# Two graph layers on one core: the order of work in the passage from the first layer to the second

## The chip, the cores and the metric

The kernel runs on one NeuronCore of a Trainium2 chip. The metric is the device time of one execution in microseconds (us), as the median of several executions. "PE" is TensorE, "DVE" VectorE, "ACT" ScalarE, "POOL" GpSimd, "SP" the engine that here only issues transfers.

## What is computed

`x` is 4096 x 256, `adj` a symmetric 0/1 matrix of 4096 x 4096 (`deg` is its row sum, at least 1). Cut to what matters:

```python
x = layernorm(x + relu(((adj + I) @ x / deg + x) @ W + b))       # layer 0
type_sum = adj @ x                                                # layer 1, x is the new x
attn_a = sigmoid(concat(type_sum, x) @ Wa.T + ba)                 # attn_b: the same with Wb, bb
h = x @ W_sa
scores = (h @ a_left)[:, None] + (h @ a_right)[None, :]
e = where(adj != 0, exp(-leaky_relu(scores, 0.01)), 0)
x_a = (e / (e.sum(1) + 1e-5)) @ h
x_b = adj @ (x @ W_gcnb) + b_gcnb
x = layernorm(x + sigmoid(attn_a * x_a + attn_b * x_b))
```

## The kernel before, in words

Each engine runs a list of instructions that is written out by hand (`nc.Block`, one function for each engine). Semaphores `S[...]` order the engines among each other; each engine takes its own list in order, so an instruction that waits holds back all that stand behind it. There are T = 32 row tiles of 128 rows, and NP = 16 pairs of them.

**Layer 0** multiplies the adjacency with `y` (`sum_rows`, L1416) tile by tile. Behind each tile come, one to three tiles later, a transpose (`t_step`), the projection of the new tile with all weights of layer 1 (`p_step`, L1451), and on ACT `proj_copies`: `q` and `ex` (columns for the scores), `gb` (the part `g` of the projection that the adjacency multiplies), and the upper half of `h`. DVE makes the lower halves (`h_lo`, L958 and L960). Values that feed TensorE are kept as two float16 parts, high and low. `g_sums` and `forms_hi` and `forms_lo` (L948 to L953) make the sums of `g` for a pair of tiles.

**Layer 1** runs over 16 steps `s`, one for each 256 columns of the adjacency, in two slots that take turns. A step has two kinds of TensorE work:
- seven products M1 to M7 of a Strassen-like scheme (`product`, L1516), 16 matmuls each, whose adjacency operand is either the panel `pan` (M3, M4) or one of five byte-wise differences of it (`difference`, L967, written by DVE to `dd`). They are made one step ahead: `free_products` M3 and M4, `outer_products` M1 and M6, `onto_products` M2 and M5, `last_product` M7. ACT and DVE read them out: `low_m34`, `low_m1`, `low_m52`, `low_m67` on ACT, `middle`, `middle_m1`, `read_52`, `add_52`, `read_67`, `add_67` on DVE. PE may not overwrite a bank before it is read (`mid_read`, `m52_read`, `m67_read`).
- four chunks of `e @ h` (`e_chunk`, L1575), 48 matmuls each. A chunk passes through `exp_chunk` (ACT, 8 exponentials, L639), `mask_chunk` (DVE, L1141), `high_chunk` (ACT, L648) and `low_chunk` (DVE, L1148); the last one raises `elow_ready`, for which the `e_chunk` waits.

At a step's end DVE (`attend`, `statistics`), POOL (`pool_bias` L456, `pool_rstd` L462 and L466) and ACT (`gates`, `gated`, `sigmoid`, `norm`) finish the rows. `act_step`, `dve_step` and `pe_step` hold the order of a step; the steps 0, 1 and 2 are written out ahead of the loop, with `ramp` and `second` marking the first two calls.

**The passage.** Before the first exponential the kernel needs a bound on the scores over all rows: `nsr` and `NM` (L1070, L1072), a transpose on PE (L1547), the maximum `NMAX` (L1101), and `slb` (L1105). PE meanwhile works on the products of panel 0, whose last pair (NP - 1) needs the last tile's `g`:

```python
pe.wait_ge(S["forms_ready"], NP)
product(0, "M3", NP - 1, NP)
product(0, "M4", NP - 1, NP)
...
pe.wait_ge(S["hlo_ready"], T)
outer_products(0, 0)
```

## Time and profile before

| what | value |
|---|---|
| median of 3 executions | 867.2 us (866.87 to 869.27) |
| the profiled execution | 867.15 us |
| its span, first to last instruction | 865.0 us |
| PE busy | 851.7 us, 98% of the span |
| DVE busy | 668.3 us, 77% |
| ACT busy | 572.9 us, 66% |
| POOL busy | 181.2 us, 21% |
| mean granted TensorE clock | 0.999 |

The 2.15 us between the span and the time of that execution lie outside the instructions. Layer 0 ends and layer 1 begins at about 315 to 341 us. A time within a row is counted from the start of the span. In a timeline row the first number is the start, the second the time until the last of the merged instructions ends, and the bracket at the end the engine's idle time before it with what released it. Instructions of one engine overlap a little, so that from one start to the next it is slightly less than the duration.

### The profile page before, as it was taken

The numbers are of one execution on the slowest core, as the hardware profiler recorded it, in microseconds if no ns is written. First come the engines' busy times: TensorE is split into PE (matmuls) and PEld (weight loads), VectorE is DVE, ScalarE is ACT, GpSimd is POOL, SyncE is SP. The second block draws the span as 40 slices with busy tenths as digits, with TensorE's granted clock in tenths as the row PEclk, the third lists the DMA queues.
The fourth block names the chain that finished last, engine by engine and source line by source line (L and its number), as shares of the span: only waits on it lengthen the run. The fifth ranks groups of instructions, "written<-read, shape, count | busy, mean of one in ns | idle before, by whom it ended". The sixth has DMA issues, their size and how long they took to land.

```text
span 865.0 us, 20467 instructions
## 1 busy us (share of the span) xinstructions
PE 851.7 (98%) x7574; PEld 753.8 (87%) x7574; DVE 668.3 (77%) x1180; ACT 572.9 (66%) x1217; POOL 181.2 (21%) x181
## 2 busy tenths in 40 slices
PE   8999999999999998999999999999999999999997
PEld 7888888888888887888888888888888888888886
DVE  6697766656665558899988988987987978978963
ACT  5774645555554238989976886876876966967831
POOL 1003232223222311013122112212122032032031
PEclk9999999999999999999999999999999999999999
DMA  9989999989895642110221021021120120120001
GB/s 316 365 297 384 366 392 365 356 313 382 305 351 205 222 153 86 56 56 2 80 80 67 13 79 67 11 79 30 48 79 24 55 79 13 65 79 0 26 25 37
DMA packets 66649, 130.01 MB, mean 150 GB/s; under 512 B 5496, under 2 KB 29088, under 8 KB 62112
## 3 DMA queue, kind: packets, MB, share of 16 engines
q1 hardware_dynamic: 57392, 120.61, 39.0%
q10 hardware_dynamic: 9200, 8.64, 3.0%
q8 instruction: 36, 0.59, 0.3%
q14 instruction: 21, 0.17, 0.1%
HBM read 99.87 MB, written 29.36 MB: 149 GB/s over the span
## 4 chain that ended last, share of the span: by engine, by line
PE 80%; DVE 9%; issue 6%; ACT 4%; POOL 1%; DMA 0%; DVEq 0%; ACTq 0%; POOLq 0%; SPq 0%
PE ps L1575 27%; PE ps L1416 25%; PE ps L1516 18%; PE ps L1451 5%; PE ps L1398 3%; DVE ec L1141 2%; DVE em L1148 2%; ACT ec L639 2%; ACT em L648 1%; DVE dd L967 1%; PE ps L1383 1%; PE ps L1436 1%; PE ps L1374 0%; POOL sc L462 0%; DMA x1r<-x_scratch 0%
## 5 line engine op out<-in xcount | busy, mean ns | idle before, releaser
L1575 PE MATMUL ps<-fb,em 128*128 128x257 f16 x3072 | 347.5, 273 | 0.8 <-DVE em L1148 0.8
L1575 PEld LDWEIGHTS ps<-fb,em 128*128 128x128 f16 x3072 | 300.4, 98 | 38.8 <-issue 1.5
L1416 PE MATMUL ps<-y,codes 128*128 128x257 f16 (+1 forms) x2048 | 237.0, 273 | 0.0
L1416 PEld LDWEIGHTS ps<-y,codes 128*128 128x128 fp8e4 x2048 | 200.2, 98 | 25.9 <-DVE y L856 0.4
L639 ACT ACTIVATE ec<-slb,nsb 128x256 f32<-128x256 f32 x512 | 211.1, 497 | 0.0
L1148 DVE SCALAR_TENSOR_TENSOR em<-ec,em 128x2048 f16<-128x2048 f32 x64 | 147.3, 2302 | 20.9 <-ACT em L648 20.9
L648 ACT ACTIVATE em<-ec 128x2048 f16<-128x2048 f32 x64 | 122.0, 1908 | 60.4 <-PE ps L1575 51.3
L1141 DVE SCALAR_TENSOR_TENSOR ec<-ec,pan 128x2048 f32<-128x2048 f32 x64 | 147.2, 2300 | 3.2 <-issue 2.8
L1516 PE MATMUL ps<-zz,dd 128*128 128x256 f16 x768 | 89.4, 273 | 0.1
L462 POOL TENSOR_TENSOR sc<-sc,sc 128x2 f32<-128x2 f32 x15 | 36.6, 2438 | 244.6 <-DVE sc L1250 244.6
L1516 PEld LDWEIGHTS ps<-zz,dd 128*128 128x128 fp8e4 x768 | 75.1, 98 | 9.1 <-issue 0.4
L514 ACT ACTIVATE codes<-strip 128x1024 uint8<-128x1024 f32 x67 | 67.1, 1044 | 1.1
L456 POOL TENSOR_TENSOR w<-w,bgb 128x512 f32<-128x512 f32 x16 | 27.7, 1732 | 177.3 <-DVE w L1208 177.3
L967 DVE SCALAR_TENSOR_TENSOR dd<-pan 128x512 uint32<-128x512 uint32 (+2 forms) x85 | 64.2, 815 | 0.0
L1516 PE MATMUL ps<-fa,pan 128*128 128x260 f16 x512 | 60.0, 274 | 1.4 <-DVE zz L953 1.1
L1516 PE MATMUL ps<-fa,dd 128*128 128x260 f16 x512 | 59.6, 274 | 1.2 <-DVE m L1160 1.1
L569 ACT ACTIVATE q<-ps,sc 128x1 f32<-128x1 f32 x32 | 11.3, 352 | 72.8 <-PE ps L1451 72.8
L1516 PEld LDWEIGHTS ps<-fa,pan 128*128 128x128 fp8e4 x512 | 49.9, 98 | 8.5 <-DVE zz L953 1.4
L1516 PEld LDWEIGHTS ps<-fa,dd 128*128 128x128 fp8e4 x512 | 49.9, 98 | 8.3 <-issue 1.7
L983 DVE TENSOR_SCALAR lnst<-ps 128x1 f32<-128x1 f32 x32 | 5.0, 155 | 62.4 <-PE ps L1416 62.4
L554 ACT ACTIVATE x1t<-ps 128x256 f16<-128x256 f32 x32 | 12.2, 383 | 60.1 <-PE ps L1436 60.1
L684 ACT ACTIVATE ot<-sg,sc 128x256 f32<-128x256 f32 x30 | 16.4, 593 | 52.1 <-POOL sc L466 52.1
(153 smaller groups left out, 827.6 us busy)
## 6 DMA issues: line engine op xcount, KB each, us to landing
strip<-in_adj_dram SPq DMA_DIRECT2D x128, 512.0 KB, 7.7
a_scratch<-codes SPq DMA_DIRECT2D x16, 1024.0 KB, 9.6
pan<-a_scratch SPq DMA_DIRECT2D x16, 1024.0 KB, 4.9
x_scratch<-x ACTq DMA_DIRECT2D x32, 128.0 KB, 5.3
x1r<-x_scratch SPq DMA_DIRECT2D x16, 256.0 KB, 2.7
h_scratch<-hst ACTq DMA_DIRECT2D x30, 136.0 KB, 5.6
out_dram<-ot SPq DMA_DIRECT2D x15, 256.0 KB, 2.2
fb<-h_scratch SPq DMA_DIRECT2D x3, 1088.0 KB, 8.7
```

The costliest lines, as they stand in the source:

```text
L456: pool.tensor_tensor(w[:], w[:], bgb[:].unsqueeze(1).broadcast_to([P, 2, D]), ALU.add).then_inc(S["bias_ready"], 1)
L462: pool.tensor_tensor(sc1[:, RS2], sc1[:, VE2], sc[:, MH2], ALU.pow).then_inc(S["yrstd_ready"], 1)
L514: act.activation(codes_of(s), strip_of(s), ACT.Copy, scale=float(EDGE - NONE), bias=float(NONE)).then_inc(S["cast_act"], 1)
L639: e_ = act.activation(ec[:, c % ER, jj, :], slb[:, slot, :], ACT.Exp, scale=-(1 - SLOPE), bias=nsb[:, jb:jb + 1])
L648: act.activation(em[:, c, 0], ec[:, c % ER], ACT.Copy, scale=MU / EDGE_VAL).then_inc(S["ehigh_ready"], 1)
L967: return dve.scalar_tensor_tensor(out=o, in0=b, scalar=0x7f7f7f7f, in1=a, op0=ALU.bitwise_and, op1=ALU.bitwise_xor)
L1141: dve.scalar_tensor_tensor(out=ec[:, c % ER], in0=ec[:, c % ER], scalar=1.0, in1=pan[:, slot, c * CH:(c + 1) * CH, :].bitcast(F8), op0=ALU ...
L1148: dve.scalar_tensor_tensor(out=em[:, c, 1], in0=ec[:, c % ER], scalar=MU / EDGE_VAL, in1=em[:, c, 0], op0=ALU.mult, op1=ALU.subtract).then ...
L1416: mm = pe.matmul(ACC(n)[:, 0:cols], codes[:, qq % SLOTS, h, jb, e * P:(e + 1) * P].bitcast(F8), y[:, jb, part, 0:cols], start=(jb == 0 and ...
L1451: mm = pe.matmul(b, x1t[:, n % 2, x_part, k * P:(k + 1) * P], wps[:, k, w_part, c0:c1], start=(k == 0 and x_part + w_part == 0), stop=(k = ...
L1516: mm = pe.matmul(ps[:, bank, 0:2 * c], a.bitcast(F8), g, start=(p == 0), stop=(p == NP - 1))
L1575: mm = pe.matmul(PH(2 * m + e)[:, 0:HC], em[:, c, e_part, i, e * P:(e + 1) * P], fb[:, jb, h_part, 0:HC], start=(jb == 0 and e_part + h_pa ...
```

## The change

It touches only the passage and the steps 0 to 2; the loop over the other steps is as before.
- PE: the last pair's matmuls are split, so that what needs only the earlier pairs (or only `fa4`, with the new semaphore `fa_ready`) stands ahead; `onto_products` of step 0 waits for one difference less; the wait for the last tile's `h_lo` moves from ahead of `outer_products(0, 0)` to ahead of the fourth `e_chunk`.
- ACT: the last tile's `gb` is copied ahead of `q` and `ex`; `slc` and the last column of `nsb` move from DVE to ACT; the last `h` moves behind `low_m34(1)`; the first `high_chunk` becomes two halves behind the fourth and the fifth exponential of chunk 1; several `high_chunk`s move ahead of an `exp_chunk`, among them the one at the head of `act_step` with `ramp`.
- DVE: the differences of the last two pairs of panel 0 move ahead of the last `g_sums`; the first mask and the first low part become two halves each; `add_52` and `add_67` of step 0, the last `h_lo`, and some differences stand later; in step 1 `mask_chunk(1, 1, 2)` stands behind the five differences of panel 2.
- POOL: its first `pool_bias` is gone, and DVE does it (`first_bias`).

```diff
@@ -467,7 +467,6 @@
                                             two(MV2, 2)[:, e, 0:1], -1.0, ALU.mult, ALU.mult)
                 p_.then_inc(S["yshift_ready"], 1)
 
-            pool_bias(0)
             with pool.Fori(0, NPAN // 2 - 1) as k:
                 for i in range(2):
                     pool_bias(k * 2 + (i + 1))
...
@@ -625,6 +624,31 @@
                 if more:
                     cast(2)
             assert next(todo, None) is None
+
+            def last_projection():
+
+                n = T - 1
+                act.wait_ge(S["proj_done"], T)
+                act.activation(gb[:, n % 2, :], BG(n)[:, 0:GC], ACT.Copy, scale=GSC).then_inc(S["g_ready"], 1)
+                act.activation(q[:, n:T], BG(n)[:, GC + 3:WG], ACT.Exp, scale=sc[:, QSC], bias=sc[:, QB]
+                               ).then_inc(S["q_ready"], 1)
+                act.activation(ex[:, n, :], BG(n)[:, GC:WG], ACT.Copy, scale=sc[:, EXS]).then_inc(S["ex_ready"], 1)
+                act.wait_ge(S["ex_ready"], T)
+                act.copy(slc[:], ex[:, :, 2]).then_inc(S["sl_ready"], 1)
+                act.activation(nsb[:, n:T], ex[:, n, 3:4], ACT.Copy, scale=-(1 - SLOPE)).then_inc(S["slb_ready"], 1)
+                forms_hi(NP - 1)
+
+            def last_h():
+
+                n = T - 1
+                act.wait_ge(S["q_ready"], T)
+                act.activation(qa[:, n:T], q[:, n:T], ACT.Copy, scale=1.0 / PROJ).then_inc(S["qa_ready"], 1)
+                act.wait_ge(S["qa_ready"], T)
+                h = h_place(n)
+                act.activation(h[:, 0, D:HC], q[:, n:T], ACT.Copy, scale=KAPPA)
+                act.activation(h[:, 0, 0:D], BH, ACT.Copy, scale=qa[:, n:T]).then_inc(S["hhi_ready"], 1)
+
+            last_projection()
 
             def exp_chunk(s, slot, c, nth=0, first=False, behind={}):
...
 
+            def first_half_high(i):
+
+                half = slice(i * CH // 2, (i + 1) * CH // 2)
+                act.wait_ge(*((S["masked"], 1) if i else (S["half_masked"], 1)))
+                h_ = act.activation(em[:, 0, 0, half], ec[:, 0, half], ACT.Copy, scale=MU / EDGE_VAL)
+                h_.then_inc(S["ehigh_ready" if i else "half_high"], 1)
+
+            def first_half_highs(u):
+
+                low_m67(u, first=True)
+                act.wait_ge(S["acc_done"], T)
+                for j in range(SLOTS):
+                    act.wait_ge(codes_out[j], 32 * len(range(j, NQ, SLOTS)))
+                first_half_high(0)
...
@@ -715,8 +754,11 @@
             def act_step(s, m, nth, ramp=False, second=False):
 
                 n = 1 - m
+                if ramp:
+                    high_chunk(s, 2)
                 exp_chunk(s + 1, n, 0, nth)
-                high_chunk(s, 2)
+                if not ramp:
+                    high_chunk(s, 2)
                 if ramp:
                     low_m34(s + 1)
                 elif second:
@@ -752,34 +794,28 @@
                 act.wait_ge(S[sem], n)
             act.wait_ge(S["slb_ready"], 2)
             exp_chunk(0, 0, 0, first=True, behind={4: low_m34, 5: low_m1, 7: lambda u: low_m52(u, first=True)})
-            exp_chunk(0, 0, 1, first=True, behind={6: lambda u: low_m67(u, first=True)})
-            act.wait_ge(S["acc_done"], T)
-            for j in range(SLOTS):
-                act.wait_ge(codes_out[j], 32 * len(range(j, NQ, SLOTS)))
-            high_chunk(0, 0, True)
+            exp_chunk(0, 0, 1, first=True, behind={4: first_half_highs, 5: lambda u: first_half_high(1)})
             act.wait_ge(S["m52_read"], 1)
             low_m34(1)
-
-            exp_chunk(0, 0, 2, first=True)
-            high_chunk(0, 1, True)
+            last_h()
+            exp_chunk(0, 0, 2, first=True, behind={5: lambda u: high_chunk(u, 1, True)})
             low_m1(1)
             for j in range(X1RING):
                 act.wait_ge(x1_out[j], 16 * T // X1RING)
-            act.wait_ge(S["proj_done"], T)
             exp_chunk(0, 0, 3, first=True)
+            high_chunk(0, 2, True)
             exp_chunk(1, 1, 0, 1)
             low_m52(1)
-            high_chunk(0, 2, True)
             high_chunk(0, 3, True)
+            high_chunk(1, 0)
             exp_chunk(1, 1, 1)
             act.wait_ge(S["arg_ready"], 1)
             act.activation(rr[:], tb[:], ACT.Exp).then_inc(S["rr_ready"], 1)
             gates(0, 0)
             gated(0, 0, first=True)
-            high_chunk(1, 0)
             low_m67(1)
+            high_chunk(1, 1)
             exp_chunk(1, 1, 2)
-            high_chunk(1, 1)
             exp_chunk(1, 1, 3)
             act_step(1, 1, 2, ramp=True)
...
 
-            def forms_lo(p):
+            def forms_lo(p, last=False):
 
                 dve.wait_ge(S["ghi_ready"], p + 1)
                 dve.tensor_tensor(fa4[:, p, 0:2, P + 2:2 * P + 4], gb[:, 0:3:2, 0:P + 2], fa4[:, p, 0:2, 0:P + 2],
                                   ALU.subtract)
-                dve.tensor_tensor(fa4[:, p, 2:4, P + 2:2 * P + 4], gb[:, 1:3, P:GC], fa4[:, p, 2:4, 0:P + 2],
-                                  ALU.subtract)
+                f_ = dve.tensor_tensor(fa4[:, p, 2:4, P + 2:2 * P + 4], gb[:, 1:3, P:GC], fa4[:, p, 2:4, 0:P + 2],
+                                       ALU.subtract)
+                if last:
+                    f_.then_inc(S["fa_ready"], 1)
...
@@ -1061,25 +1099,18 @@
             x1t_lo(6)
             forms_lo(2)
             cast(2)
-            for n in range(SPREAD + 1, T + 3):
+            for n in range(SPREAD + 1, T + 2):
                 more = n // PT + 1 < NQ and n < T
                 if n - 1 < T:
                     degree(n - 1)
-                if n == T + 2:
-                    dve.wait_ge(S["ex_ready"], T)
-                    dve.tensor_scalar(nsr[:], ex[:, :, 3], -1.0, None, ALU.mult).then_inc(S["nsr_ready"], 1)
-                    dve.wait_ge(S["nsr_ready"], 1)
-                    dve.tensor_reduce(sc[:, NM], nsr[:], AX, ALU.max).then_inc(S["nsr_max"], 1)
-                    dve.tensor_copy(slc[:], ex[:, :, 2]).then_inc(S["sl_ready"], 1)
...
                 if n - 1 < T:
                     stats(n - 1)
-                if n % 2 == 0 and n < T + 2:
+                if n % 2 == 0:
                     forms_lo((n - 3) // 2)
                 if more:
...
             assert next(todo, None) is None
+            for op in DIFF_ORDER:
+                difference(0, op, NP - 2, NP).then_inc(S["diff_ready"], 1)
+            dve.wait_ge(S["ex_ready"], T - 1)
+            dve.tensor_scalar(nsr[:, 0:T - 1], ex[:, 0:T - 1, 3], -1.0, None, ALU.mult).then_inc(S["nsr_ready"], 1)
+            dve.tensor_scalar(nsb[:, 0:T - 1], ex[:, 0:T - 1, 3], -(1 - SLOPE), None, ALU.mult)
+            dve.wait_ge(S["nsr_ready"], 1)
+            dve.tensor_reduce(nsr[:, T - 1:T], nsr[:, 0:T - 1], AX, ALU.max).then_inc(S["nsr_ready"], 1)
             g_sums(dve, NP - 1)
-            dve.tensor_scalar(nsb[:], ex[:, :, 3], -(1 - SLOPE), None, ALU.mult).then_inc(S["slb_ready"], 1)
-
+            dve.wait_ge(S["ex_ready"], T)
+            dve.wait_ge(S["nsr_ready"], 2)
+            dve.scalar_tensor_tensor(out=sc[:, NM], in0=ex[:, T - 1, 3:4], scalar=-1.0, in1=nsr[:, T - 1:T],
+                                     op0=ALU.mult, op1=ALU.max).then_inc(S["nsr_max"], 1)
             dve.wait_ge(S["nmt_done"], 1)
             dve.tensor_reduce(sc[:, NMAX], ps[:, 5, P:2 * P], AX, ALU.max).then_inc(S["nmax_ready"], 1)
             for m in range(2):
...
-            for op in DIFF_ORDER:
-                difference(0, op, NP - 2, NP).then_inc(S["diff_ready"], 1)
+            forms_lo(NP - 1, last=True)
 
             def row_ends():
 
-                h_lo(T - 1)
                 dve.wait_ge(S["slt_done"], 1)
                 dve.tensor_scalar(slrow[:], ps[0:T, 5, 0:P], sc[0:T, NMAX], None, ALU.min
@@ -1147,6 +1184,29 @@
                 gate(dve, S["ehigh_ready"], s * NCH + c + 1, "passed_dve")
                 dve.scalar_tensor_tensor(out=em[:, c, 1], in0=ec[:, c % ER], scalar=MU / EDGE_VAL, in1=em[:, c, 0],
                                          op0=ALU.mult, op1=ALU.subtract).then_inc(S["elow_ready"], 1)
+
+            def first_half_mask(i):
+
+                half = slice(i * CH // 2, (i + 1) * CH // 2)
+                dve.wait_ge(S["exp_done"], 1)
+                dve.scalar_tensor_tensor(out=ec[:, 0, half], in0=ec[:, 0, half], scalar=1.0,
+                                         in1=pan[:, 0, half, :].bitcast(F8), op0=ALU.min, op1=ALU.mult
+                                         ).then_inc(S["masked" if i else "half_masked"], 1)
+
+            def first_half_low(i):
+
+                half = slice(i * CH // 2, (i + 1) * CH // 2)
+                dve.wait_ge(*((S["ehigh_ready"], 1) if i else (S["half_high"], 1)))
+                l_ = dve.scalar_tensor_tensor(out=em[:, 0, 1, half], in0=ec[:, 0, half], scalar=MU / EDGE_VAL,
+                                              in1=em[:, 0, 0, half], op0=ALU.mult, op1=ALU.subtract)
+                if i:
+                    l_.then_inc(S["elow_ready"], 1)
+
+            def first_bias():
+
+                dve.wait_ge(S["comb_ready"], 1)
+                dve.tensor_tensor(w[:], w[:], bgb[:].unsqueeze(1).broadcast_to([P, 2, D]), ALU.add
+                                  ).then_inc(S["bias_ready"], 1)
 
             def some_differences(u, slot, ops, done=NPROD):
...
@@ -1318,35 +1378,41 @@
             middle(0)
             middle_m1(0)
             some_differences(1, 1, DIFF_ORDER[0:2], done=4)
-            mask_chunk(0, 0, 0)
+            first_half_mask(0)
             read_67(0)
+            first_half_mask(1)
             row_ends()
             read_52(0, first=True)
+            for i in range(2):
+                first_half_low(i)
+            mask_chunk(0, 0, 1)
+            some_differences(1, 1, DIFF_ORDER[2:4], done=6)
             for i in range(HRING):
                 dve.wait_ge(h_out[i], 16 * len(range(i, T - 2, HRING)))
             add_52(0, first=True)
             add_67(0)
-            low_chunk(0, 0)
-            mask_chunk(0, 0, 1)
-            some_differences(1, 1, DIFF_ORDER[2:], done=NPROD + 1)
             middle(1)
             low_chunk(0, 1)
             mask_chunk(0, 0, 2)
+            some_differences(1, 1, DIFF_ORDER[4:], done=NPROD + 1)
             middle_m1(1)
+            h_lo(T - 1)
+            low_chunk(0, 2)
             mask_chunk(0, 0, 3)
-            low_chunk(0, 2)
+            mask_chunk(1, 1, 0)
+            low_chunk(0, 3)
+            low_chunk(1, 0)
             row_factors()
-            low_chunk(0, 3)
-            mask_chunk(1, 1, 0)
-            sums_52(1)
-            low_chunk(1, 0)
+            first_bias()
+            read_52(1)
+            mask_chunk(1, 1, 1)
+            add_52(1)
             denominators()
-            mask_chunk(1, 1, 1)
             sums_67(1)
-            mask_chunk(1, 1, 2)
             low_chunk(1, 1)
             dve.wait_ge(panel_in[0], 32)
             some_differences(2, 0, DIFF_ORDER)
+            mask_chunk(1, 1, 2)
             mask_chunk(1, 1, 3)
             low_chunk(1, 2)
...
@@ -1542,23 +1608,26 @@
             pe.wait_ge(S["g_ready"], T - 1)
             pe.wait_ge(S["diff_ready"], NDIFF)
             product(0, "M2", 0, early, bank=FIRST_52[1])
-            pe.wait_ge(S["g_ready"], T)
+            pe.wait_ge(S["diff_ready"], 2 * NDIFF)
+            product(0, "M1", early, NP - 1)
+            product(0, "M6", early, NP - 1)
+            pe.wait_ge(S["ex_ready"], T)
             pe.wait_ge(S["nsr_max"], 1)
             pe.transpose(ps[:, 5, P:2 * P], sc[:, NM].broadcast_to([P, P]), ident[:]).then_inc(S["nmt_done"], 1)
             product(0, "M5", 0, early, bank=FIRST_52[0])
             pe.wait_ge(S["sl_ready"], 1)
             pe.wait_ge(S["nmax_ready"], 1)
             pe.transpose(ps[0:T, 5, 0:P], slc[:], ident[:]).then_inc(S["slt_done"], 1)
-            pe.wait_ge(S["forms_ready"], NP)
+            pe.wait_ge(S["fa_ready"], 1)
             product(0, "M3", NP - 1, NP)
             product(0, "M4", NP - 1, NP)
-            pe.wait_ge(S["diff_ready"], NDIFF + 1)
-            product(0, "M1", early, NP)
-            pe.wait_ge(S["diff_ready"], NDIFF + 2)
-            product(0, "M6", early, NP)
-            pe.wait_ge(S["diff_ready"], 2 * NDIFF)
-            product(0, "M2", early, NP, bank=FIRST_52[1])
-            product(0, "M5", early, NP, bank=FIRST_52[0])
+            product(0, "M2", early, NP - 1, bank=FIRST_52[1])
+            product(0, "M5", early, NP - 1, bank=FIRST_52[0])
+            pe.wait_ge(S["forms_ready"], NP)
+            product(0, "M1", NP - 1, NP)
+            product(0, "M6", NP - 1, NP)
+            product(0, "M2", NP - 1, NP, bank=FIRST_52[1])
+            product(0, "M5", NP - 1, NP, bank=FIRST_52[0])
...
@@ -1622,15 +1691,22 @@
                 e_chunk(s, m, 3)
                 last_product(s, m)
 
-            pe.wait_ge(S["hlo_ready"], T)
             outer_products(0, 0)
             pe.wait_ge(S["m52_read"], 1)
             pe.wait_ge(S["slrow_ready"], 1)
             for c in range(NCH):
                 pe.wait_ge(fb_in[c], 16)
+                if c == NCH - 1:
+                    pe.wait_ge(S["hlo_ready"], T)
                 e_chunk(0, 0, c)
-                if c < 2:
-                    (onto_products, last_product)[c](0, 0)
+                if c == 0:
+                    pe.wait_ge(S["mid_read"], 3)
+                    pe.wait_ge(S["diff_ready"], 3 * NDIFF - 1)
+                    product(1, "M2")
+                    product(1, "M5")
+                if c == 1:
+                    pe.wait_ge(S["diff_ready"], 3 * NDIFF)
+                    last_product(0, 0)
             e_chunk(1, 1, 0)
             free_products(1, 1, 2)
             e_chunk(1, 1, 1)
```

## Rows read from the trace of the kernel before

**Rows 1.** The page: the span and PE's total (us, share, instructions).
```profile
span 865.0 us, 20467 instructions
PE 851.7 (98%) x7574; PEld 753.8 (87%) x7574; DVE 668.3 (77%) x1180; ACT 572.9 (66%) x1217; POOL 181.2 (21%) x181
```

**Rows 2.** Busy time by stretch: length, PE, PEld, DVE, ACT, POOL, clock, DMA.
```profile
458.88:859.00 400.12, 399.84 (x3632) 355.29 (x3632) 332.97 (x427) 286.51 (x565) 81.64 (x52) 1.00 0.14 47
```

**Rows 3.** Timeline of PE, from the last projection to step 3.
```profile
323.39 1.49 PE L1451 MATMUL ps<-wps,x1t 128*128 128x262 f16 x12
...
329.33 0.40 PE L1516 MATMUL ps<-fa,pan 128*128 128x260 f16 x2 [1.14 <-DVE zz L953]
...
330.86 1.95 PE L1516 MATMUL ps<-fa,pan 128*128 128x260 f16 x16 [0.24 <-DVE m L1160]
...
340.93 5.44 PE L1575 MATMUL ps<-fb,em 128*128 128x257 f16 x48 [0.80 <-DVE em L1148]
...
415.35 3.66 PE L1516 MATMUL ps<-zz,dd 128*128 128x256 f16 x32
...
458.88 3.71 PE L1516 MATMUL ps<-fa,dd 128*128 128x260 f16 x32 [1.15 <-DVE m L1160]
```

**Rows 4.** The chain that ended last, 377 to 459 us: start, us, what.
```profile
398.68 0.79 DVE em L1148
...
432.22 2.64 POOL sc L462
...
458.15 0.35 DVE m L1160
```

**Rows 5.** Timeline of ACT, 324 to 382 us.
```profile
324.92 0.35 ACT L569 ACTIVATE q<-ps,sc 128x1 f32<-128x1 f32 x1 [2.47 <-PE ps L1451]
...
327.91 1.69 ACT L639 ACTIVATE ec<-slb,nsb 128x256 f32<-128x256 f32 x4
...
371.22 6.48 ACT L639 ACTIVATE ec<-slb,nsb 128x256 f32<-128x256 f32 x16
377.61 1.90 ACT L648 ACTIVATE em<-ec 128x2048 f16<-128x2048 f32 x1
...
381.81 1.91 ACT L648 ACTIVATE em<-ec 128x2048 f16<-128x2048 f32 x1 [2.05 <-DVE ec L1141]
```

**Rows 6.** Timeline of DVE, 330 to 415 us.
```profile
330.38 0.43 DVE L1160 TENSOR_TENSOR m<-ps,lc 128x260 f32<-128x260 f32 x1 [0.42 <-ACT lc L691]
...
335.29 0.42 DVE L1200 TENSOR_TENSOR s<-ps,lc 128x256 f32<-128x256 f32 x1
335.63 0.15 DVE L958 SCALAR_TENSOR_TENSOR fb<-q,fb 128x1 f16<-128x1 f32 x1
...
336.10 0.33 DVE L1115 TENSOR_SCALAR slrow<-ps,sc 32x128 f32<-32x128 f32 x1
...
337.10 0.23 DVE L1189 TENSOR_TENSOR sc<-s,m 128x2 f32<-128x2 f32 x2 [0.28 <-DVE s L1177]
...
338.38 2.28 DVE L1148 SCALAR_TENSOR_TENSOR em<-ec,em 128x2048 f16<-128x2048 f32 x1
340.59 3.36 DVE L1141 SCALAR_TENSOR_TENSOR ec<-ec,pan 128x2048 f32<-128x2048 f32 x1
...
354.74 2.29 DVE L1148 SCALAR_TENSOR_TENSOR em<-ec,em 128x2048 f16<-128x2048 f32 x1 [1.09 <-ACT em L648]
...
364.69 2.29 DVE L1148 SCALAR_TENSOR_TENSOR em<-ec,em 128x2048 f16<-128x2048 f32 x1 [1.13 <-ACT em L648]
...
379.40 2.28 DVE L1141 SCALAR_TENSOR_TENSOR ec<-ec,pan 128x2048 f32<-128x2048 f32 x1
...
400.89 0.68 DVE L1241 SCALAR_TENSOR_TENSOR sg<-sg,x1r 128x512 f32<-128x512 f32 x1
...
414.26 4.17 DVE L967 SCALAR_TENSOR_TENSOR dd<-pan 128x512 uint32<-128x512 uint32 x5
```

**Rows 7.** Timeline of POOL, 319 to 342 us.
```profile
338.65 3.14 POOL L456 TENSOR_TENSOR w<-w,bgb 128x512 f32<-128x512 f32 x1 [19.04 <-DVE w L1208]
```

More of the change, by code:

```diff
@@ L232, in build @@
             "sl0_out", "ex_ready", "alpha_ready", "slb_ready", "masked", "exp_done", "ehigh_ready", "elow_ready",
-            "diff_ready", "prod_done", "low_m34", "low_m1", "low_m52", "low_m67", "mid_read", "m52_read", "m67_read",
+            "fa_ready", "half_masked", "half_high", "diff_ready", "prod_done", "low_m34", "low_m1", "low_m52", "low_m67", "mid_read", "m52_read", "m67_read",
             "comb_ready", "ext_ready", "bias_ready", "echunk_done", "tile_done", "epsr_ready",
@@ L1063, in _ @@
             cast(2)
-            for n in range(SPREAD + 1, T + 3):
+            for n in range(SPREAD + 1, T + 2):
                 more = n // PT + 1 < NQ and n < T
@@ L1067, in _ @@
                     degree(n - 1)
-                if n == T + 2:
-                    dve.wait_ge(S["ex_ready"], T)
-                    dve.tensor_scalar(nsr[:], ex[:, :, 3], -1.0, None, ALU.mult).then_inc(S["nsr_ready"], 1)
-                    dve.wait_ge(S["nsr_ready"], 1)
-                    dve.tensor_reduce(sc[:, NM], nsr[:], AX, ALU.max).then_inc(S["nsr_max"], 1)
-                    dve.tensor_copy(slc[:], ex[:, :, 2]).then_inc(S["sl_ready"], 1)
-                if n < T + 2:
-                    h_lo(n - 3)
+                h_lo(n - 3)
                 if n - 1 < T:
@@ L1105, in _ @@
             dve.tensor_scalar(slb[:], slb[:], sc[:, NMAX], None, ALU.min).then_inc(S["slb_ready"], 1)
-            forms_lo(NP - 1)
-            for op in DIFF_ORDER:
-                difference(0, op, NP - 2, NP).then_inc(S["diff_ready"], 1)
+            forms_lo(NP - 1, last=True)
             def row_ends():
-                h_lo(T - 1)
                 dve.wait_ge(S["slt_done"], 1)
```

## The prediction

> **What bounds the kernel now.** I read the page first. PE is busy for 851.7 of 865.0 us [rows 1], so no order of work can win more than about 13 us. PE's work itself is the same before and after, matmul for matmul. So I looked for PE's idle time from the passage on, in its timeline [rows 3]: 1.14 us ahead of the last pair (for `zz`), 0.24 (for `middle`), 0.80 ahead of the first `e_chunk` (for the first low part), and then 1.15 at 458.88, far behind the passage, again for a `middle`. From there to 859 us PE is busy for 399.84 of 400.12 us [rows 2]. So the end of the kernel is the start at 458.88 plus a constant, and the change is worth what it moves that start.
>
> Then I asked the chain of waits what holds 458.88, and this decides my forecast [rows 4]. Between 381.81 and 458.88 the chain does not touch PE. It runs through ACT (from the `high_chunk` at 381.81 on [rows 5], ACT without a pause of note to the `high_chunk` that releases DVE's low part at 398.68), then DVE to 432 us, then POOL's `pool_rstd` (432.22, 2.64 us), ACT, and DVE to `middle` at 458.15. PE has only 1.15 us to spare against that chain. Two clocks run side by side: PE's, and the ACT and DVE chain's. A gain counts only if both move; if only PE's moves, PE waits later.
>
> **PE's clock.** The first copy of ACT behind the last projection stays at 324.92 [rows 5]. With `gb` ahead of `q` (0.35) and `ex`, the `g_sums` and the forms come about 0.5 us earlier. `slb` does not: it needs `ex`, now behind `gb`, then NM, transpose and maximum. The shorter last reduction and the moved `slc` pay that back, so the first exponential starts at about 327.75 instead of 327.91 (before, the end of `forms_hi` held it). Four exponentials at 0.40 each (sixteen took 6.48 [rows 5]) bring ACT to `low_m34` at 329.35. PE, which before started the last pair at 329.33, is now through with it by then and no longer late. So `middle(0)` starts about 0.5 us earlier than its 330.38 [rows 6], at 329.87, and PE goes on at 330.3 instead of 330.86 [rows 3]: of PE's 1.4 us of idle time, 1.0 stays, now in one piece ahead of `product(1, "M3")`.
>
> PE's next 80 matmuls, less the wait for `h_lo` that stood among them (some 0.3 us), bring it to the first `e_chunk` at 339.1. The first low part decides next. DVE does two differences and the first half mask by 333.6 and then waits in `read_67`, because `low_m67` needs M7 finished: 330.3 + 32 matmuls at 0.11 = 333.8, 334.0 with the last one's tail; copy and hand-over 0.5: 334.55, against 335.29 before [rows 6]. From there: `read_67` 0.34, a half mask 1.13 (half of the 2.21 from 338.38 to 340.59 and a small fixed part; bounds 1.1 and 1.3), `slrow` 0.25, `read_52` 0.33, two half lows 2.26: DVE is free at 338.85, its data ready at 338.95. Before, with the `h_lo` (0.47 from 335.63 to 336.10) and the additions (1.28 from 337.10 to 338.38) ahead, that was 338.38 + 2.28 = 340.66 [rows 6]. PE starts its `e_chunk` at 339.25 instead of 340.93 [rows 3], 1.7 us earlier. Up to the end of step 1 each chunk's low part is ready ahead of PE by this sum (the closest is chunk 3 of step 0, 359.8 for 360.8), so PE's clock stands at -1.65 us.
>
> **The clock of ACT and DVE.** DVE did in 41.1 us, from 340.59 until `mask_chunk(1, 1, 3)` ended at 381.7 [rows 6], what it now starts at 338.85. The differences: the mask at 340.59 took 3.36 where others take 2.28, while POOL's `pool_bias` ran (338.65, 3.14 us [rows 7]); without POOL that is -1.08. In sentences that the sum can do without: the Trainium skill (SBUF — State Buffer, "Who interferes with whom") says that a DVE instruction with two SBUF inputs and a POOL instruction that reads SBUF lock each other out, and the trace agrees with 1.08 us. The moved bias costs DVE 0.55 (512 elements; the nearest row is `statistics`' 0.68, 400.89 [rows 6]; bounds 0.45 and 0.7). The two waits for ACT at 354.74 and 364.69 (1.09 and 1.13 [rows 6]) go: by my count the new order leaves 0.4 of them, ahead of `low_chunk(0, 2)`. The additions and the last `h_lo` move in: +1.28 and +0.47. In all 41.1 - 1.08 + 0.55 - 2.22 + 0.4 + 1.28 + 0.47 = 40.5: `mask_chunk(1, 1, 3)` ends at 379.35, 2.3 us earlier than before. So far the change does well.
>
> But the change swaps two things that meet here. `mask_chunk(1, 1, 2)` now stands behind the five differences, directly ahead of `mask_chunk(1, 1, 3)`, so it ends at 379.35 - 2.2 = 377.15; before it stood ahead of `low_chunk(1, 1)`. And ACT now puts `high_chunk(1, 2)`, which needs that mask, ahead of `exp_chunk(2, 0, 0)`. Before, ACT ran the two exponential chunks from 371.22 to 377.6 without a pause and took the `high_chunk` at 377.61 [rows 5] with its mask done. Now ACT has its last exponential done at 374.5 (by a count of its own list: the `high_chunk` ahead of `exp_chunk(1, 1, 2)` is released by a mask that ends at 366.3, 1.8 for it, 6.4 for two exponential chunks) and stands idle for 2.6 us until 377.2. Then, with nothing left to overlap: `high_chunk` 1.8, `exp_chunk` 3.2, `low_m34` 0.25, and it is at the `high_chunk(1, 3)` at 382.45, which before started at 381.81 [rows 5]. From there to `low_chunk(2, 1)` of DVE at 398.68 [rows 4] nothing changes (16.87 us, ACT's own work). So this clock comes out at 399.3, **+0.65 us**, although DVE was 2.3 us ahead.
>
> **What is late next.** Behind `low_chunk(2, 1)` DVE worked without a pause of note; its differences for step 3 began at 414.26 [rows 6], now 414.9. PE wants the first of them for `outer_products` at 415.35 - 1.65 = 413.7 [rows 3] and gets it at 415.6: a new idle time of some 2 us, at L1516, that eats PE's gain. From there PE has its old place plus 0.3. POOL and ACT follow DVE's +0.65, and `middle` starts at about 458.7, so PE goes on at 459.5. The sum against the profiled execution is 867.15 + 0.65 = 867.8; the median shown lies 0.05 above that execution: **867.9 us**. This is inside 0.3% (2.6 us), about what a measurement of this kernel can tell from no change.
>
> The other edits cost nothing that lasts: the last `h` is ready near 351 and wanted at 360.8; the panel's transfer is issued with the mask of chunk 3, about 1.7 us later than before, and lands about 10 us before its use; `pool_bias(1)` still takes its 1.08 from DVE, in the same stretch as before, and is in the sum.
>
> **The rivals.**
> - *DVE's lead survives.* If mask 2 is ready in time for ACT, or my sum for DVE is 3 us too long, the later chain moves with PE's clock: -1.65, and the 1.15 at 458.88 shrinks too, at most -2.8: 864.4 to 865.6. For it: DVE is 2.3 us ahead at 379 by my own sum, and the half instructions and the bias could be shorter. Against it: the 22.1 us of ACT work in a row from `high_chunk(1, 2)` on are rows, not guesses.
> - *Slower by a clock drop.* PE would stand idle for 1.0 us at 329.3 and 2 us at 413.7, longer than any gap in this stretch before. If the granted clock fell to 1.2 GHz behind one, an `e_chunk` of 5.28 us would take 10.5, and the end would be 5 us later beyond DVE's cover: 872. Against it: gaps of 1.14 and 1.15 us left the clock at 1.00 [rows 2, 3]. It decides only if the gap is long enough. The Trainium skill (TensorE: Matmul & The Clock Gate, "HAM oscillation — how this bites in real kernels") warns of idle gaps in which the clock drops to half; no row here shows one.
> - *The chain gets later than I count.* A further wait of ACT on DVE ahead of 377.2 (halves at 1.3, bias at 0.7) adds up to 1 us: 869.0. It is the upper end of my own case.
> - *Nothing moves.* The two clocks cancel exactly: 867.2, inside my own case.
>
> **How the numbers follow.** My case (ACT idle ahead of `high_chunk(1, 2)`, end between -0.8 and +1.9 us): 0.74, own range 866.4 to 869.1. DVE's lead survives: 0.19, of which 0.07 reach beyond 2.6 us. Clock drop: 0.03; a longer delay of the chain that I don't see: 0.04. So faster by over 0.3% 0.07, within 0.86, slower 0.07. The range takes my case and the upper half of the first rival: 865.2 to 869.6.
>
> **What would show it.** Right: PE's first `e_chunk` at 339.3 and its idle time ahead of it gone; DVE's first mask of chunk 1 at 2.28 us; ACT idle for 2 to 3 us, released by a mask (L1141's successor), ahead of a `high_chunk` near 377; low part (2, 1) at 399.3; a new gap of PE of about 2 us near 414, released by a difference. Wrong: no such gap near 414, or the gap at 458 gone; then the first rival holds. A granted clock under 1.00 near 330 or 415 would be the second.

## The result and the profile after

The changed kernel takes 868.6 us in the median of 22 executions, the kernel before 867.5 beside it: ratio 1.0013, 95% interval 1.0007 to 1.0019. That is 1.1 us more, clear of noise, and under the 0.3% of the forecast's middle class. I had forecast +0.65 us. The trace after is that of one execution of 868.78 us; where I give a number of a trace below, it comes from one execution of each kernel.

The page of the kernel after, span and totals:

```profile
span 866.7 us, 20471 instructions
PE 851.2 (98%) x7574; PEld 753.7 (87%) x7574; DVE 668.2 (77%) x1183; ACT 573.9 (66%) x1220; POOL 178.5 (21%) x180
```

The timeline of PE after (start, length, instruction, idle time before it and its releaser), in the lines that answer to [rows 3]:

```profile
323.92 1.49 PE L1517 MATMUL ps<-wps,x1t 128*128 128x262 f16 x12
...
331.00 1.95 PE L1582 MATMUL ps<-fa,pan 128*128 128x260 f16 x16 [0.89 <-DVE m L1220]
...
340.17 5.44 PE L1644 MATMUL ps<-fb,em 128*128 128x257 f16 x48 [0.21 <-DVE em L1200]
...
416.76 3.65 PE L1582 MATMUL ps<-zz,dd 128*128 128x256 f16 x32 [2.26 <-DVE dd L1005]
...
460.54 3.71 PE L1582 MATMUL ps<-fa,dd 128*128 128x260 f16 x32 [1.39 <-DVE m L1220]
```

One thing first: the last projection starts at 323.92 here and at 323.39 before. The code up to there is the same, and in the traces of this study that start lies between 322.9 and 324.6 whatever the kernel. So 0.53 of the 1.7 us between the two spans has nothing to do with the change, and I count every time from now on from the start of the last projection.

Counted so, the first `e_chunk` came 1.29 us earlier (16.25 for 17.54), and then PE lost it all: 2.26 us at 416.76, waiting for a difference (L1005), where before it waited for nothing, and again 1.39 at 460.54 for `middle` (1.15 before). That last start, the one that sets the end, comes at 136.62 for 135.49: **+1.13 us**, which is the measured 1.1. Why DVE was late is in ACT's timeline after, for [rows 5]:

```profile
369.26 6.48 ACT L663 ACTIVATE ec<-slb,nsb 128x256 f32<-128x256 f32 x16
378.21 1.91 ACT L672 ACTIVATE em<-ec 128x2048 f16<-128x2048 f32 x1 [2.47 <-DVE ec L1178]
380.03 3.29 ACT L663 ACTIVATE ec<-slb,nsb 128x256 f32<-128x256 f32 x8
383.22 0.35 ACT L730 COPY lc<-ps 128x260 f32<-128x260 f32 x1
383.48 1.91 ACT L672 ACTIVATE em<-ec 128x2048 f16<-128x2048 f32 x1
```

After two exponential chunks ACT stands still for 2.47 us until the mask of chunk 2 is done, and only then come the `high_chunk`, the third exponential chunk and `high_chunk(1, 3)`. Before, ACT ran from 371.22 to 379.5 without that pause [rows 5]. DVE's timeline after shows both sides of it, in the lines for [rows 6]:

```profile
335.43 0.42 DVE L1260 TENSOR_TENSOR s<-ps,lc 128x256 f32<-128x256 f32 x1 [1.06 <-ACT lc L752]
...
339.83 2.27 DVE L1178 SCALAR_TENSOR_TENSOR ec<-ec,pan 128x2048 f32<-128x2048 f32 x1
...
364.09 0.69 DVE L1208 TENSOR_TENSOR w<-w,bgb 128x512 f32<-128x512 f32 x1
...
371.71 4.17 DVE L1005 SCALAR_TENSOR_TENSOR dd<-pan 128x512 uint32<-128x512 uint32 x5
375.80 4.48 DVE L1178 SCALAR_TENSOR_TENSOR ec<-ec,pan 128x2048 f32<-128x2048 f32 x2
...
383.46 2.29 DVE L1178 SCALAR_TENSOR_TENSOR ec<-ec,pan 128x2048 f32<-128x2048 f32 x1 [0.90 <-ACT ec L663]
...
400.35 2.29 DVE L1185 SCALAR_TENSOR_TENSOR em<-ec,em 128x2048 f16<-128x2048 f32 x1 [1.42 <-ACT em L672]
```

The mask at 339.83 takes 2.27 us, not 3.36. The five differences (371.71) stand ahead of the two masks (375.80). The masks end at 380.28, which is 1.9 us earlier than before counted from the projection; but DVE then waits for ACT, and at 400.35 it is 1.14 us later.

### The profile page after: what moved, and what is told of

Read it like the earlier page. It is cut to its first block, busy times and chain, and to the rows that moved or that the text cites. A ratio compares the mean times of both kernels' runs of the same rounds, so it can differ in the third digit from the quotient of the medians.

```text
span 866.7 us, 20471 instructions
## 1 busy us (share of the span) xinstructions
PE 851.2 (98%) x7574; PEld 753.7 (87%) x7574; DVE 668.2 (77%) x1183; ACT 573.9 (66%) x1220; POOL 178.5 (21%) x180
## 4 chain that ended last, share of the span: by engine, by line
PE 78%; DVE 10%; issue 5%; ACT 4%; DMA 2%; POOL 1%; SPq 0%; DVEq 0%; ACTq 0%; POOLq 0%
PE ps L1644 27%; PE ps L1482 25%; PE ps L1582 18%; PE ps L1517 5%; DVE em L1185 2%; DVE ec L1178 2%; PE ps L1464 2%; ACT em L672 1%; DMA xs<-in_x_dram 1%; ACT ec L663 1%; DVE dd L1005 1%; PE ps L1502 1%; DVE sc L859 1%; PE ps L1449 0%; POOL sc L462 0%
## 5 line engine op out<-in xcount | busy, mean ns | idle before, releaser
L672 ACT ACTIVATE em<-ec 128x2048 f16<-128x2048 f32 x63 | 120.2, 1908 | 59.4 <-PE ps L1644 50.2
L1185 DVE SCALAR_TENSOR_TENSOR em<-ec,em 128x2048 f16<-128x2048 f32 x63 | 143.9, 2286 | 20.2 <-ACT em L672 20.2
L1178 DVE SCALAR_TENSOR_TENSOR ec<-ec,pan 128x2048 f32<-128x2048 f32 x63 | 143.8, 2285 | 5.1 <-ACT ec L663 2.5
L1005 DVE SCALAR_TENSOR_TENSOR dd<-pan 128x512 uint32<-128x512 uint32 (+2 forms) x85 | 65.3, 827 | 0.0
L456 POOL TENSOR_TENSOR w<-w,bgb 128x512 f32<-128x512 f32 x15 | 24.8, 1653 | 178.1 <-DVE w L1268 178.1
```

Source lines behind the costliest of these rows:

```text
L456: pool.tensor_tensor(w[:], w[:], bgb[:].unsqueeze(1).broadcast_to([P, 2, D]), ALU.add).then_inc(S["bias_ready"], 1)
L672: act.activation(em[:, c, 0], ec[:, c % ER], ACT.Copy, scale=MU / EDGE_VAL).then_inc(S["ehigh_ready"], 1)
L1005: return dve.scalar_tensor_tensor(out=o, in0=b, scalar=0x7f7f7f7f, in1=a, op0=ALU.bitwise_and, op1=ALU.bitwise_xor)
L1178: dve.scalar_tensor_tensor(out=ec[:, c % ER], in0=ec[:, c % ER], scalar=1.0, in1=pan[:, slot, c * CH:(c + 1) * CH, :].bitcast(F8), op0=ALU ...
L1185: dve.scalar_tensor_tensor(out=em[:, c, 1], in0=ec[:, c % ER], scalar=MU / EDGE_VAL, in1=em[:, c, 0], op0=ALU.mult, op1=ALU.subtract).then ...
```

## The experiments

My theory: two clocks, PE's own and that of ACT and DVE; the second sets the end, and one meeting in it (late mask, early `high_chunk`) throws the gain away. Rivals: the loss lies elsewhere in DVE's work; or PE's total work sets the end. "M2 of step 4" is the start of PE's `onto_products` near 458, the one that sets the end; both columns of times count from the last projection.

| kernel | ratio, 95% interval | first `e_chunk` | M2 of step 4 |
|---|---|---|---|
| before | 1 | 17.54 | 135.49 |
| after | 1.0013 (1.0007 to 1.0019) | 16.25 | 136.62 |
| e1_exp_first | 0.9984 (0.9975 to 0.9993) | 16.29 | 134.02 |
| e2_mask_first | 0.9985 (0.9976 to 0.9994) | 16.24 | 134.01 |
| e11_both_undone | 0.9980 (0.9971 to 0.9989) | 16.28 | 134.05 |
| e9_before_high_first | 1.0001 (0.9992 to 1.0010) | 17.54 | 135.54 |
| e10_before_both | 1.0038 (1.0024 to 1.0051) | 17.55 | 138.92 |
| e3_before_bias | 0.9989 (0.9980 to 0.9998) | 17.54 | 134.65 |
| e4_before_m52 | 0.9983 (0.9974 to 0.9992) | 17.53 | 134.18 |
| e5_pe_8 | 1.0002 (0.9993 to 1.0011) | 17.54 | 135.49 |
| e6_pe_24 | 1.0016 (1.0006 to 1.0025) | 17.53 | 136.69 |
| e7_whole_chunk | 1.0034 (1.0023 to 1.0046) | 17.46 | 137.78 |
| e8_exp_m52 | 0.9965 (0.9952 to 0.9977) | 16.25 | 132.47 |
| e12_early_reads | 0.9956 (0.9943 to 0.9970) | 15.86 | 132.09 |

### The meeting, undone in the changed kernel

e1, in `act_step`:

```diff
-                if ramp:
-                    high_chunk(s, 2)
                 exp_chunk(s + 1, n, 0, nth)
-                if not ramp:
-                    high_chunk(s, 2)
+                high_chunk(s, 2)
```

> The changed kernel with one edit undone: at the head of the ramp step ACT takes exp_chunk(2, 0, 0) again ahead of high_chunk(1, 2). My theory (ACT's 2.5 us of idle time ahead of that high_chunk makes the whole later chain late): the idle time is filled by the exponentials, high_chunk(1, 3) starts about 2.4 us earlier (near 381 instead of 383.5), low_chunk(2, 1) too, PE's 2.3 us gap near 414 ahead of outer_products goes, and the end comes 2.4 us earlier than in the changed kernel: 1.3 us under the kernel before (0.9985), with a gap of PE of about 1.1 us left near 458. Rival (the loss lies in the front of the passage, in DVE's own later work, and this order only moves the idle time about): the time stays 1.1 us above the kernel before.

e2, in DVE's list:

```diff
+            mask_chunk(1, 1, 2)
             dve.wait_ge(panel_in[0], 32)
             some_differences(2, 0, DIFF_ORDER)
-            mask_chunk(1, 1, 2)
             mask_chunk(1, 1, 3)
```

> The changed kernel with the other half of the same meeting undone: DVE takes mask_chunk(1, 1, 2) again ahead of the five differences of panel 2; ACT's order stays as changed. My theory: the mask is then ready when ACT has done exp_chunk(1, 1, 3) (near 375.8), ACT's idle time falls from 2.5 to about 0.2 us, and the end comes about 2.2 us earlier than in the changed kernel, 1.1 us under the kernel before (0.9987). DVE may wait up to 0.8 us for the exponentials of that mask, which costs the end nothing. Rival (DVE is the one that is late, so its order doesn't matter for the sum): 1.1 us above the kernel before, as the changed kernel.

e11 has both edits.

> The changed kernel with both parts of the meeting undone. My theory: either one alone cures the wait (each measured 1.3 to 1.5 us under the kernel before), so both together give the same, 0.9983 to 0.9985. Rival (two separate losses): the gains add, 4 us under the kernel before (0.9955).

Each alone takes 2.6 us off the changed kernel (136.62 to 134.0; I expected 2.4 and 2.2), and both together no more. So it is one loss, and it needs both sides. ACT's timeline of e1 shows the pause filled:

```profile
369.64 9.68 ACT L663 ACTIVATE ec<-slb,nsb 128x256 f32<-128x256 f32 x24
379.23 1.90 ACT L672 ACTIVATE em<-ec 128x2048 f16<-128x2048 f32 x1
```

and that of e2 the mask in time:

```profile
368.89 6.48 ACT L663 ACTIVATE ec<-slb,nsb 128x256 f32<-128x256 f32 x16
375.27 1.90 ACT L672 ACTIVATE em<-ec 128x2048 f16<-128x2048 f32 x1
```

### The meeting, put into the kernel before

e9 moves only ACT's `high_chunk(1, 2)` ahead of `exp_chunk(2, 0, 0)`; e10 also puts `mask_chunk(1, 1, 2)` behind the five differences.

> The kernel before with ACT's part of the meeting alone: high_chunk(1, 2) ahead of exp_chunk(2, 0, 0); DVE's order as before, with mask_chunk(1, 1, 2) ahead of the differences. My theory (the order costs only together with the late mask): the mask is done near 373.2 and ACT gets there at 374.4, so it does not wait, and the high part of chunk 3 stays at 381.8 behind its own mask: no change (1.0000, 0.2 us either way). Rival (ACT's order is bad by itself): 1 us or more longer.

> The kernel before with both parts of the meeting: mask_chunk(1, 1, 2) behind the five differences on DVE, and high_chunk(1, 2) ahead of exp_chunk(2, 0, 0) on ACT; nothing else of the change. My theory: the mask ends near 379.9, ACT stands idle from 374.4 to 380, and with 22.1 us of ACT's work from there low_chunk(2, 1) starts near 402.1 instead of 398.7: the end comes 3.4 us later (1.0039), with a gap of PE of 1 to 2 us near 416. Rival (PE or another wait behind absorbs part of it): 1 us or less.

e9: no change. e10: +3.43 us at M2 of step 4, for 3.4 expected (its median is 2.9 us over that of the kernel before), with a long pause of ACT:

```profile
379.69 1.91 ACT L648 ACTIVATE em<-ec 128x2048 f16<-128x2048 f32 x1 [5.42 <-DVE ec L1144]
```

The pause of 5.42 us stands in place of the one of 2.05 us that ACT had at 381.81 [rows 5]; the difference is the 3.4 us. So these two moves of the change cost 3.4 us by themselves. In the changed kernel they cost 2.6 (136.62 less 134.02): DVE comes to the mask earlier there, and the pause of 2.47 us stands in place of none in e1. The rest of the change wins 1.4 (e11), and the sum is the loss of 1.1. The mask's move alone was not put into the kernel before; in the changed kernel e1 is that case, and it costs nothing there. PE's timeline of e10 holds something I come back to:

```profile
407.08 3.71 PE L1519 MATMUL ps<-fa,pan 128*128 128x260 f16 x32 [0.74 <-DVE s L1182]
...
418.23 5.24 PE L1519 MATMUL ps<-zz,dd 128*128 128x256 f16 x32 [2.16 <-DVE dd L970]
423.31 5.44 PE L1578 MATMUL ps<-fb,em 128*128 128x257 f16 x48
```

### Which clock sets the end

e5 and e6 put more work on PE in the kernel before (8 and 24 small transposes of 0.11 us), and e4 takes DVE's late wait away. The edit of e5 and e6, shown with e5's number, and behind it that of e4:

```diff
                 if c < 2:
                     (onto_products, last_product)[c](0, 0)
+                if c == 1:
+                    for _ in range(8):
+                        pe.transpose(ps[:, 7, 384:512], ident[:], ident[:])
```

> The kernel before with 8 transposes more on PE (of the unit matrix into an unused part of a bank, 0.11 us each, 0.9 us in all) ahead of the third e_chunk of step 0. It measures PE's slack against the chain of ACT and DVE. My theory (1.15 us of slack at 458): the time stays, the gap at 458 shrinks to about 0.3 us. Rival (every microsecond of PE counts): 0.9 us longer (1.0010).

> As the run with 8, with 24 transposes more on PE (2.6 us). My theory: the first 1.15 us are free, the gap at 458 is gone, and 1.5 us remain (1.0017). Rival (every microsecond of PE counts): 2.6 us longer (1.0030).

```diff
-                    norm(s - 2)
                     low_m52(s)
+                    norm(s - 2)
```

> The kernel before with an edit of the loop: ACT takes low_m52(s) ahead of norm(s - 2). It is there to test the chain behind the passage: at 437 us ACT waits 5.4 us for POOL in norm, and DVE waits 2.15 us for the low_m52 behind it. My theory (that chain sets PE's start at 458.88): DVE comes 2.2 us earlier, PE's gap of 1.15 us goes, and the end comes 1.1 us earlier (0.9987), no more, as PE has no other gap. Rival (the end is set by something else, as PE's total work from the passage on): no change.

PE in e5, at the start that sets the end, with a gap still there though PE worked 0.9 us more:

```profile
458.89 3.71 PE L1516 MATMUL ps<-fa,dd 128*128 128x260 f16 x32 [0.54 <-DVE m L1160]
```

The gap fell by 0.61 us and not by 0.9. The other 0.28 went into two small waits of PE further ahead (0.18 us before the third `e_chunk` of step 0, 0.10 before the second of step 1), which are gone in e5.

In e6 the end moved by 1.2 us of the 2.6 (1.4 by the medians), near the 1.5 expected, but partly by another way than I wrote. PE's delay reached ACT through the product that `low_m1` reads, so the chain itself became later, as ACT's timeline of e6 shows:

```profile
387.20 0.27 ACT L696 COPY lc<-ps 128x128 f32<-128x128 f32 x1 [1.10 <-PE ps L1516]
```

Before, ACT waited for POOL in `norm`, and DVE for the `low_m52` behind it (ACT's timeline, then DVE's):

```profile
437.15 1.09 ACT L684 ACTIVATE ot<-sg,sc 128x256 f32<-128x256 f32 x2 [5.36 <-POOL sc L466]
438.15 0.35 ACT L706 COPY lc<-ps 128x260 f32<-128x260 f32 x1
...
438.65 0.43 DVE L1179 TENSOR_TENSOR s<-ps,lc 128x260 f32<-128x260 f32 x1 [2.15 <-ACT lc L706]
```

In e4 ACT does `low_m52` and then waits for POOL:

```profile
431.91 0.35 ACT L706 COPY lc<-ps 128x260 f32<-128x260 f32 x1
437.36 1.09 ACT L684 ACTIVATE ot<-sg,sc 128x256 f32<-128x256 f32 x2 [5.10 <-POOL sc L466]
```

DVE's `read_52` follows its low part without the 2.15 us pause, PE's gap at M2 of step 4 is gone, and the end comes 1.3 us earlier in the trace and 1.5 by the medians (1.1 expected). The bracket of 1.15 us understates that gap: from one start to the next PE lost 1.31 us there (457.57, which is 5.28 behind the `e_chunk` at 452.29, to 458.88). The passage is untouched in e4. PE had slack and the chain had none.

### Parts of the change

e3 is the kernel before with `pool_bias(0)` taken out and `first_bias()` behind `row_factors()` on DVE.

> The kernel before with one part of the change alone: the first bias on DVE (behind row_factors) instead of POOL. My theory: the mask of chunk 1 takes 2.28 us instead of 3.36, the bias costs DVE 0.6 later, DVE and ACT come 0.45 us earlier from there on, and as their chain sets the end, the end comes 0.4 to 0.5 us earlier (0.9995). Rival (PE's clock sets the end): no change, PE's gap at 458 stays 1.15 us or shrinks without gain. Second rival (the stretched mask has another cause than POOL): it stays at 3.36 us, and the kernel loses 0.6 us.

DVE's timeline of e3, beside 3.36 in [rows 6]:

```profile
340.75 2.28 DVE L1140 SCALAR_TENSOR_TENSOR ec<-ec,pan 128x2048 f32<-128x2048 f32 x1
...
357.10 0.68 DVE L1153 TENSOR_TENSOR w<-w,bgb 128x512 f32<-128x512 f32 x1
```

The stretched mask was POOL's doing: 1.08 us back for 0.6. The gain was 0.84 us in the trace, 0.4 more than the sum. Those 0.4 appear in step 1 between `read_67` and `add_67`, where DVE now goes on 0.56 us after the start of `read_67` instead of 0.92. That is so in every kernel here without POOL's first bias, the changed one too, and its cause stays open.

e7 is the changed kernel with the first chunk whole again.

> The changed kernel with the first chunk whole again (one mask, one high part behind chunk 1's exponentials, one low part), all else as changed. My theory: the halves serve PE's first e_chunk only. Without them the first low part waits for one whole mask and one whole high part in a row: the first e_chunk starts 1 to 2 us later than in the changed kernel (near 341.5), a gap of 1 to 2 us of PE opens ahead of it, DVE and ACT come about 1 us later as well, since DVE's next mask stands behind that low part, and the end is 0.5 to 1.5 us above the changed kernel. Rival (DVE and ACT make up for it in the waits that they have until 377): the end stays that of the changed kernel, because only the late chain counts.

```profile
337.84 2.29 DVE L1185 SCALAR_TENSOR_TENSOR em<-ec,em 128x2048 f16<-128x2048 f32 x1 [2.33 <-ACT em L672]
```

Without halves DVE stands still for 2.33 us, and PE's first `e_chunk` comes 1.21 us later than in the changed kernel. M2 of step 4 comes 1.16 us later too: DVE did not catch up behind it. By the medians e7 is 1.7 us slower than the changed kernel, a little over the 1.5 that I expected at most, and the traced execution is the fastest of its seven; the trace can't show where the others lost more. The halves serve both clocks, not PE's alone.

### The version that beats both

e8 joins e1's edit and e4's to the changed kernel; e12 also moves the first reads of the product banks:

```diff
-            exp_chunk(0, 0, 0, first=True, behind={4: low_m34, 5: low_m1, 7: lambda u: low_m52(u, first=True)})
+            exp_chunk(0, 0, 0, first=True, behind={3: low_m34, 4: low_m1, 6: lambda u: low_m52(u, first=True)})
```

> The changed kernel with exp_chunk(2, 0, 0) ahead of high_chunk(1, 2) again and with low_m52(s) ahead of norm(s - 2) in the loop. My theory (two clocks: the late chain of ACT and DVE, and PE's own, which the passage moved 1.2 us earlier): with both late waits gone the end is set by PE alone, 2.4 us under the kernel before (0.9973), no gap near 414 nor near 458. Rival (the two edits cure the same wait): 1.2 to 1.3 us under the kernel before.

> The version with exp_chunk(2, 0, 0) first and low_m52 ahead of norm, with one more edit: low_m34, low_m1 and low_m52 of the first product set stand one exponential earlier on ACT. It is aimed at PE's last gap in the passage (0.90 us, for middle). My theory (PE alone sets the end of that version, so what its gap loses counts in full): middle starts 0.4 us earlier, PE's gap falls from 0.9 to 0.5 us, the end comes 0.4 us earlier, 3.3 us under the kernel before (0.9961). Rival (the first e_chunk waits for the first low part, which is not earlier): the gap moves to the first e_chunk, no change against 0.9965.

In e8 PE has no gap from the first `e_chunk` to step 4, and in e12 the gap for `middle` fell from 0.90 to 0.49. PE's timeline of e12:

```profile
330.50 1.95 PE L1579 MATMUL ps<-fa,pan 128*128 128x260 f16 x16 [0.49 <-DVE m L1217]
...
339.67 5.44 PE L1641 MATMUL ps<-fb,em 128*128 128x257 f16 x48 [0.21 <-DVE em L1197]
...
455.90 3.71 PE L1579 MATMUL ps<-fa,dd 128*128 128x260 f16 x32
```

e12 takes 863.8 us beside 867.3 of the kernel before: 0.9956 (0.9943 to 0.9970), the fastest here. Against e8 it is 0.38 us ahead in the trace, as expected; the two intervals overlap, so that step is seen in the trace only. e8 gained 3.0 us where I expected 2.4. The first `e_chunk` gives 1.29 of it, the gap near 458 gives 1.31 counted from start to start, and the rest are three small waits of the kernel before in steps 0 and 1 (0.18, 0.18 and 0.10 us), which went as well.

## Why the prediction was right, point by point

- **The end is the start of M2 near 458 plus a constant.** Right. It is 1.13 us later in the trace, the time 1.1.
- **PE's clock.** The first `e_chunk` was to come 1.7 us earlier and came 1.29 earlier. The mis-sized term is the hand-over at `low_m67`: `read_67` started at 334.90 (335.43 less 0.53) for 334.55. PE's run with M7 in it started 0.17 later than in my sum (330.47 for 330.3), and `read_67` came 0.2 later after it than I allowed.
- **The clock of ACT and DVE.** The stretched mask, gone: right. The bias takes 0.69, or 0.60 from its start to the next, for 0.55. `mask_chunk(1, 1, 3)` ended at 379.75 for 379.35, the same 0.35 to 0.4 carried on. That the stretch between came out at 40.45 for 40.5 is partly luck: DVE waited 0.75 us for ACT in it (0.58 and 0.17) where I had left 0.4, and the 0.36 between `read_67` and `add_67`, which I did not foresee, paid that back.
- **The meeting.** Right in place and size: ACT idle for 2.47 us (2.6 forecast), 22.14 us from that `high_chunk` to DVE's low part at 400.35 (22.1 forecast). My count of ACT's own list was 0.7 us short (its exponentials ended at 375.21 for 374.5), which cost nothing, as the mask ended later still. e1, e2, e10 and e11 show that this meeting is the cause, and e9 that ACT's half of it is harmless alone.
- **PE's new gap near 414.** Right: 2.26 us, released by a difference.
- **The sum.** +0.65 forecast, +1.13 in the trace. Of the missing 0.48, 0.35 arose by `read_67`; the rest is in small terms behind it, as `read_52` (0.40 for 0.33) and the hand-over from the mask to ACT (0.13 for 0.05).
- **Rival, DVE's lead survives.** Not in this kernel, but it is what e1 and e2 are: 1.4 us under the kernel before.
- **Rival, clock drop.** Not in the profiled execution: the granted clock was 1.00 on both sides of the 2.26 us gap. In e10 it happened (below), and the mean clocks below suggest that it happened in other executions of the changed kernel. I gave it 0.03, too little for a drop, and I was wrong about its price too: in e10 ACT's and DVE's chain covered it.

## What to carry to other kernels

Follow the chain of waits back from the last gap of the engine that seems to bound the kernel. If the chain does not touch that engine for a long stretch (here 77 us), a gap of that engine closed ahead of the stretch is worth nothing unless the chain comes earlier too. Two harmless reorderings on two engines can be harmful together: check each moved consumer against the place of its producer in the other engine's new list. And measure slack by adding work: 8 small transposes told that PE had a microsecond to spare (ratio 1.0002, 0.9993 to 1.0011).

## What the runs showed of the hardware

In e10 PE waited 0.74 us at 407 and 2.16 us at 416, and the 32 matmuls behind took 5.24 us where the same 32 take 3.65. The rows by stretch of e10 (length, PE, PEld, DVE, ACT, POOL, granted clock, DMA) show why:

```profile
410.00:416.00 6.00, 6.00 (x56) 5.15 (x53) 6.00 (x3) 5.87 (x15) 6.00 (x2) 1.00 0.00 0
416.00:418.00 2.00, 0.07 (x1) 0.00 (x0) 1.82 (x5) 2.00 (x3) 0.50 (x2) 1.00 0.00 0
418.00:420.00 2.00, 1.77 (x9) 1.27 (x10) 2.00 (x3) 2.00 (x6) 1.21 (x1) 0.53 0.00 0
420.00:422.00 2.00, 2.00 (x13) 1.46 (x12) 2.00 (x4) 2.00 (x7) 0.00 (x0) 0.62 0.61 198
422.00:424.00 2.00, 2.00 (x21) 1.79 (x19) 2.00 (x2) 2.00 (x7) 0.00 (x0) 1.00 0.88 265
```

The granted clock fell to 0.53 of 2.4 GHz, near its lower level of 1.2 GHz, behind the gap, and was full again by 422. In the changed kernel a gap of 2.26 us left it at 1.00, and so did 2.25 us in e7. So a gap of this length can bring the clock down and need not; e10 also had the gap of 0.74 us ahead of it, and each of these is one profiled execution. The mean clock of whole executions points the same way: it was 0.998 or 0.999 in every execution of the kernel before whose clock is on record, and in every one of the versions without a gap of 2 us near 416, and 0.996 or 0.997 in 13 of 22 of the changed kernel, 2 of 7 of e7 and 3 of 5 of e10. A mean does not say where the clock fell. The 13 took 868.62 us in the median and the other 9 took 868.55, so the end did not pay there either.

In e10's trace the price was 1.6 us of PE time, and the end did not pay it: `middle` ended at 461.63, PE's `e_chunk` at 462.04, and with the 0.39 us that pass between a `middle` and PE's start in the kernel before, the chain alone would have given the same 462.0.

The Trainium skill (SBUF — State Buffer, "Who interferes with whom") says that a DVE instruction with two SBUF inputs and a POOL instruction that reads SBUF contend for a shared port, which one of them holds alone. e3 agrees: the mask fell from 3.36 to 2.28 us when POOL's bias went. What I had not expected is how much the price depends on what DVE does then. In the changed kernel POOL's bias of step 1 (369.51, 3.41 us) stretches the five differences to 4.17 us. In e2 its end falls for the most part into DVE's wait for ACT, and the mask and the differences behind it take 2.38 and 3.08, so the bias costs DVE 0.1 us instead of 1.1:

```profile
372.33 2.38 DVE L1178 SCALAR_TENSOR_TENSOR ec<-ec,pan 128x2048 f32<-128x2048 f32 x1 [0.90 <-ACT ec L663]
374.63 3.08 DVE L1005 SCALAR_TENSOR_TENSOR dd<-pan 128x512 uint32<-128x512 uint32 x5
```
